# Causal and full attention of a small decoder: ScalarE copies a closed half's sums out of PSUM, VectorE transposes the copy, TensorE waits for the copy alone

## The reference

```python
q, k, v = ...                                             # layer 1: x @ W + b; layer 2: per head x_h @ W.T
scores = jnp.einsum('bhqd,bhkd->bhqk', q, k) * scale      # causal: masked above the diagonal
probs = jax.nn.softmax(scores, axis=-1)
ctx = jnp.einsum('bhqk,bhkd->bhqd', probs, v).transpose(0, 2, 1, 3).reshape(b, s, d)
return ctx @ Wo + bo
```

## Time and profile before

| | |
|---|---|
| runs, median (lowest to highest) | 2594.25 us (2590.24 to 2604.80) |
| profiled execution, own time | 2600.38 us |
| its span, mean granted clock of TensorE | 2598.6 us, 0.908 |
| TensorE busy | 2276.5 us, 88% |
| VectorE busy | 1431.6 us, 55% |
| ScalarE busy | 1125.8 us, 43% |
| GpSimd busy | 659.1 us, 25% |
| causal stage, exponentials | 355 to 637 us |
| full stage, exponentials | 1200 to 1551 us |

### The profile page before, as it was taken

The page is one execution under the profiler, slowest core; times in us unless marked ns, Lnnn a source line. Parts: engine busy times, 40 slices in busy tenths (PEclk is TensorE's granted clock), DMA queues, the critical chain, the costliest instruction groups (busy, mean ns, idle before and its releaser), DMA issues. The chain is left out here.

```text
span 2598.6 us, 41898 instructions
## 1 busy us (share of the span) xinstructions
PE 2276.5 (88%) x15210; PEld 1512.3 (58%) x15210; DVE 1431.6 (55%) x3533; ACT 1125.8 (43%) x1923; POOL 659.1 (25%) x868
## 2 busy tenths in 40 slices
PE   1489999998889999949999998799998798699996
PEld 1387754444436699934444444367665545589995
DVE  6825366785565221158999965666566555511114
ACT  6533335655433011134777774421443334234444
POOL 6110132222110133322011012000356310245551
PEclk8689978988998999966999999789999898699998
DMA  5200122330112189933222101031111210689996
GB/s 195 64 5 1 27 48 46 50 50 18 30 34 106 39 309 334 329 108 54 34 41 35 26 7 46 2 91 58 33 27 19 57 18 2 217 293 354 355 343 235
DMA packets 86208, 268.89 MB, mean 103 GB/s; under 512 B 25306, under 2 KB 43858, under 8 KB 69740
## 3 DMA queue, kind: packets, MB, share of 16 engines
q1 hardware_dynamic: 70324, 233.10, 29.4%
q0 software_dynamic: 15680, 33.12, 4.0%
HBM read 207.36 MB, written 23.94 MB: 89 GB/s over the span
## 5 line engine op out<-in xcount | busy, mean ns | idle before, releaser
L1616 ACT ACTIVATE prob<-st_ps 128x1024 f32<-128x1024 f32 x448 | 412.9, 933 | 220.0 <-PE st_ps L1483 218.7
L1636 DVE TENSOR_REDUCE cmax<-ring 128x1 f32<-128x512 f32 x640 | 401.2, 682 | 43.7 <-PE ring L1491 41.4
L3082 PE MATMUL A<-xbT,w 128*128 128x128 f32 x2512 | 301.3, 276 | 0.3 <-issue 0.3
L3082 PEld LDWEIGHTS A<-xbT,w 128*128 128x128 f32 x2512 | 291.4, 193 | 0.8 <-issue 0.5
L1530 PE MATMUL acc<-prob,v 128*32 128x256 f32 (+2 forms) x3200 | 267.0, 408 | 13.4 <-DVE byq L1674 12.3
L3326 DVE COPY yb<-C 128x256 f32<-128x256 f32 x118 | 50.1, 425 | 283.7 <-PE C L3090 277.5
L2999 POOL DMA_INDIRECT y_rows_dram<-yb,dst x118 | 116.4, 986 | 323.8 <-DVE yb L3326 320.7
L3090 PE MATMUL C<-w,hid 128*128 128x256 f32 x632 | 149.5, 380 | 0.0
L1483 PE MATMUL st_ps<-qst,kst 64*128 64x512 f32 (+3 forms) x560 | 137.3, 489 | 7.3 <-DMA qst<-parts 3.1
L2986 POOL DMA_INDIRECT xb<-x_rows_dram,src x118 | 115.1, 976 | 99.9 <-DVE src L3296 64.6
L1632 DVE CUSTOM_DVE_ANT_0 masked<-ring,causal_wide 128x512 bf16<-128x512 f32 (+3 forms) x256 | 112.5, 487 | 47.8 <-PE ring L1491 46.9
(11 more groups left out here) (475 smaller groups left out, 4491.7 us busy)
## 6 DMA issues: line engine op xcount, KB each, us to landing
w<-L3f_W_dram SPq DMA_DIRECT2D x79, 1026.0 KB
w<-L1f_W_dram SPq DMA_DIRECT2D x39, 1536.0 KB
room<-y_rows_dram SPq DMA_DIRECT2D x8, 1024.0 KB, 10.4
kst<-parts SPq DMA_DIRECT2D x120, 64.0 KB, 2.4
qst<-parts SPq DMA_DIRECT2D x120, 64.0 KB, 2.4
gate<-L2f_gates_dram SPq DMA_DIRECT2D x5, 1536.0 KB, 7.1
first<-parts SPq DMA_DIRECT2D x96, 64.0 KB, 2.4
qT<-dense SPq DMA_DIRECT2D x84, 64.0 KB, 2.4
```

The source lines that it names most:

```text
L1616: act.activation(prob[:, step % PROBS, 2 * p:2 * p + 2, 0:n], st_ps[:, p, :, 0:n], ACT.Exp, scale=scale)\
L1636: dve.tensor_reduce(cmax[:, a, t:t + 1, k0 // CH], spot(key)[:, 0:k1 - k0], AX.X, ALU.max)\
L3082: mm = pe.matmul(A[:, j % 2 * 2 + a, f * TB:(f + 1) * TB], up_w(w[:, j % WB], a, k, f), xbT[:, j % 2, k, :], start=(k == 0), stop=(k == KT ...
```

## The change

A new tile `sums` (128x512 float32, in SBUF) and a new semaphore `taken`. After the two exponentials of an iteration ScalarE waits for the closing step's products and for the previous transpose, and copies `acc` to `sums`. VectorE's transpose waits for that copy and reads `sums`. TensorE's first `weigh` of the next half waits for the copy in place of the transpose. Two closings that come after the last step are taken at the end of ScalarE's list.

```diff
+            sums = sbuf(nc, inner, "sums", [P, CH])
             byq = sbuf(nc, inner, "byq", [P, CH])
...
                         if hc:
-                            pe.wait_ge(s.turned, hc)
+                            pe.wait_ge(s.taken, hc)
...
+                def take(step):
+                    hc = step // nS * HALVES + half_of[step % nS]
+                    act.wait_ge(s.av_done, step + 1)
+                    if hc:
+                        act.wait_ge(s.turned, hc)
+                    act.activation(sums[:, :], acc[:, :], ACT.Copy).then_inc(s.taken, 1)
+
...
                         act.activation(prob[:, step % PROBS, 2 * p:2 * p + 2, 0:n], st_ps[:, p, :, 0:n], ACT.Exp, scale=scale)\
                            .then_inc(s.exp_done, 1)
+                    if closing(step - LAG):
+                        take(step - LAG)
                     if step + LEAD < NC:
                         extras(step + LEAD)
+                for step in range(NS - LAG, NS):
+                    if closing(step):
+                        take(step)
...
                 def turned(step):
                     hc = step // nS * HALVES + half_of[step % nS]
-                    dve.wait_ge(s.av_done, step + 1)
+                    dve.wait_ge(s.taken, hc + 1)
                     if hc:
                         dve.wait_ge(s.divided, hc)
-                    dve.transpose(byq[:, :], acc[:, :]).then_inc(s.turned, 1)
+                    dve.transpose(byq[:, :], sums[:, :]).then_inc(s.turned, 1)
```

More of the change, by code:

```diff
@@ L1251, in stacked_attention @@
             s = sems(nc, "q_cleared k_cleared split stacked0 stacked1 stacked2 wo_loaded ones_ready act_filled act_freed dve_filled dve_freed neg_ready c_loaded0 c_loaded1 s_ready exp_done "
-                         "cleaned av_done turned inverted divided evacuated max_cleared hi_kept valued")
+                         "cleaned av_done taken turned inverted divided evacuated max_cleared hi_kept valued")
             st_ps = psum(nc, inner, "st_ps", [P, 2, 2, CH])
```

## The result

| | before | after |
|---|---|---|
| runs, median (lowest to highest) | 2593.87 us (2588.86 to 2604.80), 7 runs | 2615.79 us (2611.63 to 2627.72), 7 runs |
| profiled execution, own time | 2600.38 us | 2611.63 us |
| its span, granted clock | 2598.6 us, 0.908 | 2609.9 us, 0.905 |

The ratio is 1.0089, 95% interval [1.0074, 1.0105]: 22 us slower. The interval is 19 to 27 us. Forecast was 2614.

What follows compares the result with a forecast made beforehand. VectorE was taken to bound the full stage and TensorE the causal one. Causal 15.25 us plus full 4.45 us gave 19.7 us over the profiled 2600.4 us, or 2614 us from the runs' median of 2594.25; range 2597 to 2630 us.

Steps and rivals of the forecast that it cites:

- the mechanism of the causal stage: 355 to 637 us: copy behind the second exponential delays VectorE's transpose, and the three-bank ring passes this to TensorE; +15.25 us.
- The hand-off after the exponentials: At each closing the copy is visible 0.58 us after the iteration's second exponential ends, if the sums are closed by then.
- First halves at full clock: Causal closings of a first half: transpose 1.28 to 1.53 us late, TensorE loses 1.3 us at each of four, 5.2 us.
- second halves: Causal closings of a second half: transpose 0.98 to 1.14 us late, 0.9 us lost at each of six, 5.4 us.
- the 0.85 of the ends: End of the causal stage: +0.2 us in the tail and +0.65 us at the last closing.
- the clock: Rival, chance 0.15: new causal stalls bring three more stretches at half clock, +31 us in all, 2626 us.
- the full stage: About 1200 to 1551 us: VectorE sets the pace, its waits add up and TensorE's gain is lost; +4.45 us.
- The term of 0.25 us per closing: Full stage: VectorE idles 0.25 us for the copy at each of 14 closings up to 1516.6 us, 3.5 us.
- The ends: Last two closings of the full stage: +0.3 us at 1536 us, and +0.65 us where the transpose follows product plus copy.
- the rival that this wait paces the stage: Full stage, chance 0.06: TensorE's wait for the transpose sets the pace; its 12.3 us go, ends cost 1.3, 2583 us.
- Hidden in the ring: Rival, chance 0.20: causal lateness counts only where TensorE itself waits, full stage even; +7 us, 2601 us.
- It does nothing: Rival, chance 0.07: ScalarE's copy and the shifted waits cancel within each stage; 2594 us.

Runs made afterwards that it cites:

- filled kernels: Kernels before and after, each with spare score products added on TensorE in the causal stage; ratios to before 0.9991 and 1.0083, causal stage 257.7 and 275.0 us.
- copy between: Changed kernel, but in the causal stage ScalarE copies between the iteration's two exponentials; ratio to before 1.0011, causal stage 256.2 us.
- ScalarE's time only: Changed kernel, but ScalarE copies a constant nobody waits for; transpose and TensorE's wait as before; ratio to before 1.0004, causal stage 258.0 us.
- causal only: Changed kernel with the change kept in the causal stage alone, full stage as before; ratio to before 1.0088, causal stage 282.2 us.
- lateness alone: Changed kernel, but TensorE waits for nothing at closings; VectorE still waits for the copy, now of a constant; causal stage 284.7 us against 261.0 before.

## Why the prediction was right, step by step

**Right: the mechanism of the causal stage.** The copy stands behind the second exponential, VectorE waits for it, and the ring passes that on. The hand-off after the exponentials was 0.52 us for 0.58, the transposes' waits 12.8 us in 13. My working has 17.8 for the same 13. First halves at full clock waited 1.33 and 1.34 us (two), second halves 0.83 to 1.00 (seven), all as predicted within 0.2. Four first halves now lie at half clock and waited 0.99 each. I had three there, with 2.06 each, and the fourth at full clock with 1.28; that is the difference. From transpose to transpose, where both kernels run at full clock, the interval that was 11.06 us became 12.26 and the next 22.96 became 23.78. The first has the effect of a second-half closing plus some 0.4 us by which the following transpose is later still; the second has the effect of a first-half closing less that. So second halves cost 0.8 us and first halves 1.2, where I had 0.9 and 1.3: 7 x 1.2 + 6 x 0.8 + 0.85 = 14 us for my 15.25, with the 0.85 of the ends taken from the forecast. The sum of both, 2.0 us a pair, is measured; its split in 1.2 and 0.8 hangs on the 0.4. The filled kernels say 11 to 12 by the stage and the same 2.0 by the pair. I took it that lateness under some 0.3 us is absorbed; the copy between, with waits of 0.2 to 0.4 us, still costs 0.3 us a pair.

**Missed: the clock, not a rival but a second term beside the waits.** I gave it 0.15, because the new stalls were shorter than the 3.11 us of the earlier trace rows. Time at half clock rose from 68 to 108 us in the causal stage. At 0.3 to 0.39 us each the 40 us more are 12 to 16 us; what the intervals and the filled kernels leave for it, of the trace's 23, is 9 to 12. Of the 22 us between medians, less 14 for the waits and 2 for the full stage, 6 are left. The split can't be made sharper than that with these runs: the waits were sized at full clock, and at half clock they are shorter. The mean clocks of the runs fit: over 35 runs of before, 0.01 less mean clock goes with 15.6 us more, over three sets of 17 with 11 to 12, and the clock is 0.9036 in the mean of the runs of after against 0.9100, which makes 7 to 10 us. This is a correlation. That the low clock comes with the wait is shown by the kernels in which the wait is gone (copy between, 43 us at half clock; ScalarE's time only, 57) and by those that have it (causal only, 111; lateness alone, 114). How short a stall is enough was not measured. The Trainium skill's rule (TensorE: Matmul & The Clock Gate, HAM oscillation) spoke for this rival. Its case is of waits for transfers; here the time at half clock rose with waits of up to 1.3 us for another engine.

**Mis-sized: the full stage.** I had 4.45 us. Measured are 2.1. The term of 0.25 us per closing came out at 0.10 (the 13 intervals up to the closing of 1516.6, 1.3 us), because VectorE arrives 0.74 us after the last product, not 0.64, and the copy is visible after 0.82, not 0.88; both small differences go the same way, and the term was their rest. The ends cost 0.8, for my 0.95. TensorE's waits at the accumulator fell in the full stage from 10.7 us to the 3.0 that the copy's line shows up to 1545 us, and it won nothing by it: the rival that this wait paces the stage is refuted.

**The sum was right partly by luck.** 19.7 us predicted, 21.9 measured between medians: one term (waits) 1 to 4 us too large, one (full) 2.3 too large, and 6 to 12 us of the clock missing. The measured stages add to 25, and the other 3 are within what a single execution varies. That the forecast fell within 2 us of the median is the errors cancelling. I also took 13 us as the least that can be told; seven runs each told 4.

**The other rivals.** "Hidden in the ring" (+7) falls by the kernel with the lateness alone: the ring of three banks passes it on. "It does nothing" falls by the result. The transposes cost 711 ns from on-chip memory and 710 from PSUM; the 65 ns less that the Trainium skill's fixed costs would give (VectorE: DVE Perf Modes, the TRN2 errata) don't show.

## What to carry to other kernels

A hand-off to another engine costs the place that it gets in that engine's list, not its duration: the same 0.6 us copy, 32 times, cost 22 us behind the second exponential; ahead of it in the causal stage it cost 2 us, which the runs can't tell from nothing. Ask of each wait added what stands behind it, and whether that frees a buffer that the bounding engine needs. Where TensorE bounds a stage, count the clock as a term of its own: with waits of 0.8 to 1.3 us on VectorE at each closing came 40 us more at half clock. And compare kernels over a stretch of the same work at the same clock: the pair told 0.3 us apart where stage times of one kernel differ by 4.

## What was not expected of the hardware

- The 128x512 transpose takes 711 to 712 ns out of on-chip memory in the kernel after (689 to 712 where it was moved) and 704 to 717 ns out of PSUM.
- A 128x512 copy out of PSUM takes 592 ns on ScalarE, like the exponential of that shape (597); when it stands between two exponentials it is 603.
- VectorE starts 0.03 us after the end of the copy that it waits for (1238.97 + 0.59 = 1239.56, start 1239.59). TensorE's product starts 0.14 to 0.15 us after it (1239.71; 457.25 + 0.62 = 457.87, start 458.01). The prediction had 0.07 for both.
- With the change the clock fell even where no transfer was awaited: 0.52 over 594 to 619 us, with the transfers' share at 0.01. From 571 to 619 us TensorE waited 1.5 us for the copy and 0.6 for maxima, and for no transfer.
- 1 us at half clock cost about 0.3 us of this stage.
